# A four-layer attention network on one core: who adds up the causal layer's softmax sums

## The reference

```python
x_ln = _ln(xs, ln1_g, ln1_b)
q = (x_ln @ wq).reshape(b, n, HEADS, DHEAD).transpose(0, 2, 1, 3)
q = q * DHEAD ** (-0.5)
kv = x_ln @ wkv
k, v = (kv[..., :DHEAD], kv[..., DHEAD:])      # one head of keys and values for 8 query heads
sim = jnp.einsum('bhid,bjd->bhij', q, k)
sim = jnp.where(causal, neg, sim)              # causal: key after query
attn = jax.nn.softmax(sim, axis=-1)
out = jnp.einsum('bhij,bjd->bhid', attn, v)
out = out.transpose(0, 2, 1, 3).reshape(b, n, INNER) @ wo
av = _ln(out + xs, ln2_g, ln2_b)
ff = _ln(av, ff_ln1_g, ff_ln1_b) @ ff_w1 + ff_b1
ff = _ln(ff, ff_ln2_g, ff_ln2_b)
ff = jax.nn.gelu(ff, approximate=False) @ ff_w2 + ff_b2
y = ff + av
```

## Time and profile before

| | |
|---|---|
| time, median of 3 runs | 1603.95 us (1603.63 to 1605.78) |
| span of the profiled execution, first to last instruction | 1601.4 us |
| time beside that span | 2.55 us, by the median |
| TensorE busy | 1359.2 us, 85% |
| VectorE busy | 1013.7 us, 63% |
| ScalarE busy | 586.2 us, 37% |
| GpSimd busy | 123.3 us, 8% |
| mean granted TensorE clock | 0.896 of 2.4 GHz |

### The profile page before, as it was taken

One profiled execution on the slowest core, in us unless ns is written; L12 is line 12 of the kernel. 1 busy time (PEld: TensorE's weight loads), 2 busy tenths in 40 slices (PEclk: granted clock), 3 DMA queues, 4 the chain that ended last, 5 costly groups with the idle time before them and its releaser, 6 DMA issues.

```text
span 1601.4 us, 21756 instructions
## 1 busy us (share of the span) xinstructions
PE 1359.2 (85%) x7584; PEld 1024.8 (64%) x7584; DVE 1013.7 (63%) x1837; ACT 586.2 (37%) x797; POOL 123.3 (8%) x314
## 2 busy tenths in 40 slices
PE   4789888859988989876988898896798798889689
PEld 3668654448776865445877776444687687545577
DVE  3656578666565657765646566776565565696655
ACT  3424234524332423533433332353343242245243
POOL 0000011210000002110000000222000000112100
PEclk8799979969978988987998997997898899899799
DMA  4000110000000020000000003000000001200000
GB/s 137 0 27 1 40 41 2 1 1 1 29 1 27 1 67 14 1 1 1 1 29 1 27 0 80 2 1 1 1 0 29 0 1 27 54 1 2 1 1 27
DMA packets 16396, 27.24 MB, mean 17 GB/s; under 512 B 2576, under 2 KB 6800, under 8 KB 16272
## 3 DMA queue, kind: packets, MB, share of 16 engines
q1 hardware_dynamic: 16272, 25.66, 5.8%
HBM read 8.61 MB, written 4.19 MB: 8 GB/s over the span
## 4 chain that ended last, share of the span: by engine, by line
issue 88%; POOL 7%; PE 4%; POOLq 0%; DVE 0%; ACT 0%
PE ring L584 4%; POOL cprobs L555 3%; POOL rstd L539 2%; POOL idle_pool L554 2%; PE ring L654 0%; PE ring L710 0%; POOLq L424 0%; POOLq L538 0%; PE ring L715 0%; ACT h_hi L944 0%; DVE y L1136 0%; POOLq L542 0%; DVE gn_nb L1202 0%; DVE gn_sc L1200 0%; DVE gn_msc L1201 0%
## 5 line engine op out<-in xcount | busy, mean ns | idle before, releaser
L1002 ACT ACTIVATE cprobs<-ring 128x1024 f32<-128x1024 f32 (+1 forms) x192 | 152.1, 812 | 204.8 <-PE ring L830 204.2
L584 PE MATMUL ring<-probsT_hi,vt_hi 128*128 128x512 f32 x384 | 157.3, 410 | 13.6 <-DVE probsT_lo L1086 13.6
L890 ACT ACTIVATE probsT_hi<-ring 128x1024 fp32r<-128x1024 f32 x96 | 98.0, 1026 | 182.1 <-PE ring L654 181.7
L1086 DVE TENSOR_TENSOR probsT_lo<-ring,probsT_hi 128x1024 fp32r<-128x1024 f32 x96 | 116.5, 1221 | 66.2 <-ACT probsT_hi L890 66.2
L806 PE MATMUL ring<-ks,qs 96*128 96x512 f32 (+3 forms) x384 | 144.0, 452 | 14.2 <-DVE part_max L1331 6.1
L584 PE MATMUL ring<-probsT_hi,vt_lo 128*128 128x512 f32 x384 | 153.1, 399 | 0.0
L584 PE MATMUL ring<-probsT_lo,vt_hi 128*128 128x512 f32 x384 | 152.6, 397 | 0.0
L1331 DVE TENSOR_REDUCE part_max<-ring 128x2 f32<-128x1024 f32 (+3 forms) x128 | 127.3, 1017 | 36.1 <-PE ring L810 17.9
L1119 DVE TENSOR_REDUCE neg_max<-ring 128x1 f32<-128x1024 f32 x96 | 116.8, 1221 | 32.7 <-PE ring L584 29.1
L830 PE MATMUL ring<-qs,ks 98*128 98x512 f32 (+3 forms) x384 | 115.0, 394 | 14.7 <-DVE part_max L1331 12.2
L539 POOL TENSOR_TENSOR rstd<-var_eps,half_neg 128x2 f32<-128x2 f32 (+1 forms) x52 | 46.2, 889 | 1026.7 <-DVE var_eps L1197 555.9
(11 more groups left out here) (218 smaller groups left out, 2670.7 us busy)
## 6 DMA issues: line engine op xcount, KB each, us to landing
qs<-q_hi SPq DMA_DIRECT2D x64, 128.0 KB, 2.3
xin<-x_dram SPq DMA_DIRECT2D x4, 1024.0 KB, 4.9
qs<-q_lo SPq DMA_DIRECT2D x32, 128.0 KB, 2.3
out_dram<-y SPq DMA_DIRECT2D x8, 512.0 KB, 3.1
qs<-max_rows SPq DMA_DIRECT2D x64, 4.0 KB
raw_L_wv<-L_wv_dram SPq DMA_DIRECT2D x2, 256.0 KB, 6.1
raw_L_woT<-L_woT_dram SPq DMA_DIRECT2D x2, 256.0 KB, 6.3
raw_L_wqT<-L_wqT_dram SPq DMA_DIRECT2D x2, 256.0 KB, 6.6
```

The costliest lines, as they stand in the source:

```text
L584: ins = mm(out, w, m, start=first and n == 0, stop=last and n == len(every) - 1)
L890: A(dst, flat(name) if src is None else src, ACT.Identity, bias=bias, scale=scale).then_inc(hi_ready, 1)
L1002: A(causal_probs(step, two, n), slot(event_name(e))[:, :, 0:n], ACT.Exp).then_inc(act_read, 1)
L1086: ins = v.tensor_tensor(dst, src, f32(hi), ALU.subtract)
```

## The change

GpSimd adds a block's probability tiles into a new SBUF tile `block_sum` (128 x 4 x 512) as ScalarE delivers them. The products with `ones` leave `values`; a new event `total`, once a block, multiplies `block_sum` with `ones` into bank 1.

- `total(k-1)` stands in the order after the third pair of `exp` of block `k`, directly before the first `values` of block `k`; that of the last block stands after the last `values`. The accumulator's unit is now closed by it, not by the last `values`, so ScalarE's copy and the six `norm` pieces come after it; the `norm` pieces go out two at a time.
- GpSimd takes per `exp` with `jt` of 1 or more: the mask, if on the diagonal, and an add. At `jt` = 1 it adds tiles 0 and 1 (and copies the first columns where tile 1 is narrower); before that it waits until the previous block's `total` has read `block_sum`. Each add waits for the one before it (`block_added`) and for its own mask or exponential.
- ScalarE waits, before it overwrites a `cprobs` buffer, for the add of four steps earlier.
- The scratch for DMA descriptors is set to 1024 bytes, which makes room for `block_sum`.

```diff
@@ causal_schedule
             base += [("exp", k, jt, pair, step) for pair in range(2)]
+            if k and jt == LAG:
+                base.append(("total", k - 1))
             if len(pending) == LAG:
                 base.append(pending.pop(0))
...
             events += [f for at, f in fill[k] if at == i]
-            if divide:
-                events.append(divide.pop(0))
-            if e[0] == "values" and e[1] < k and e[2] == TPH * (blocks[k - 1][1] + 1) - 1:
+            events += divide[:2]
+            divide = divide[2:]
+            if e[0] == "total":
                 divide = norm(k - 1)
...
-    return events + pending + norm(len(blocks) - 1) + [...]
+    return events + pending + [("total", len(blocks) - 1)] + norm(len(blocks) - 1) + [...]
@@ gpsimd
+                        if jt == 0:
+                            continue
+                        total = block_sum[:, 2 * two:2 * two + 2, :]
+                        if jt == 1:
+                            if kk:
+                                wait_filled(pool, b, event_name(("total", kk - 1)))
+                            elif two == 0:
+                                wait_filled(pool, b, event_name(("q2", 1)))
+                        if e in diagonal:
+                            pool.wait_ge(diag_masked, b * DIAG + diag_no[event_name(e)] + 1)
+                        else:
+                            wait_read(pool, b, event_name(e))
+                        new = causal_probs(step, two, n)
+                        if jt == 1:
+                            old = causal_probs(step - 1, two, HALF)
+                            if n < HALF:
+                                pool.tensor_tensor(total[:, :, 0:HALF - n], old[:, :, 0:HALF - n],
+                                                   ones[:, 0:1].unsqueeze(1).broadcast_to([P, 2, HALF - n]), ALU.mult)
+                            pool.tensor_tensor(total[:, :, HALF - n:HALF], old[:, :, HALF - n:HALF], new,
+                                               ALU.add).then_inc(block_added, 1)
+                        else:
+                            pool.wait_ge(block_added, b * ADDS + added[kk, jt - 1, two] + 1)
+                            pool.tensor_tensor(total[:, :, HALF - n:HALF], total[:, :, HALF - n:HALF], new,
+                                               ALU.add).then_inc(block_added, 1)
@@ tensor
+                    if e[0] == "total":
+                        pe.wait_ge(block_added, b * ADDS + added[kk, TPH * (ib + 1) - 1, 1] + 1)
+                        for a in range(4):
+                            last = mm(acc[DH * a:DH * (a + 1), 1, :], ones[:, 0:DH], block_sum[:, a, :],
+                                      start=True, stop=True)
+                        last.then_inc(ring_filled, 1)
...
-                        for bank, w in ((0, v2[:, jt, :]), (1, ones[:, 0:DH])):
-                            for a in range(4):
-                                last = mm(acc[DH * a:DH * (a + 1), bank, HALF - n:HALF], w,
-                                          causal_probs(step, a // 2, n)[:, a % 2, :],
-                                          start=jt == 0, stop=jt == last_jt)
-                        if jt == last_jt:
-                            last.then_inc(ring_filled, 1)
+                        for a in range(4):
+                            mm(acc[DH * a:DH * (a + 1), 0, HALF - n:HALF], v2[:, jt, :],
+                               causal_probs(step, a // 2, n)[:, a % 2, :], start=jt == 0, stop=jt == last_jt)
@@ scalar
+                        if step >= 4:
+                            _, k4, j4, _, _ = step_of[step - 4]
+                            act.wait_ge(block_added, b * ADDS + added[k4, max(j4, 1), two] + 1)
                         A(causal_probs(step, two, n), slot(event_name(e))[:, :, 0:n],
                           ACT.Exp).then_inc(act_read, 1)
-                    elif e[0] == "values" and e[2] == TPH * (blocks[e[1]][1] + 1) - 1:
+                    elif e[0] == "total":
@@ kernel
-    nc = _bacc.Bacc("TRN2", target_bir_lowering=False, num_devices=1)
+    nc = _bacc.Bacc("TRN2", target_bir_lowering=False, num_devices=1, dynamic_dma_scratch_size=1024)
```

More of the change, by code:

```diff
@@ L130, in causal_schedule @@
             events += [f for at, f in fill[k] if at == i]
-            if divide:
-                events.append(divide.pop(0))
-            if e[0] == "values" and e[1] < k and e[2] == TPH * (blocks[k - 1][1] + 1) - 1:
+            events += divide[:2]
+            divide = divide[2:]
+            if e[0] == "total":
                 divide = norm(k - 1)
         assert not divide
-    return events + pending + norm(len(blocks) - 1) + [(e, part) for e in FEED_FORWARD for part in (1, 2)]
+    return events + pending + [("total", len(blocks) - 1)] + norm(len(blocks) - 1) + [(e, part) for e in FEED_FORWARD for part in (1, 2)]
 def evenly(events, places):
@@ L193, in ring_units @@
             for e in causal_schedule():
-                if e[0] == "norm" or len(e) == 2 and e[0] not in FILLS + ("shift",):
+                if e[0] == "norm" or len(e) == 2 and e[0] not in FILLS + ("shift", "total"):
                     continue
@@ L197, in ring_units @@
                     held = True
-                    if e[2] == TPH * (causal_blocks()[e[1]][1] + 1) - 1:
-                        accumulated(event_name(e), "act", (0, 1))
-                        held = e[1] + 1 < len(causal_blocks())
+                elif e[0] == "total":
+                    accumulated(event_name(e), "act", (0, 1))
+                    held = e[1] + 1 < len(causal_blocks())
                 else:
@@ L244, in build @@
     DIAG = len(diagonal)
+    added = {e[1:4]: i for i, e in enumerate(e for e in schedule if e[0] == "exp" and e[2])}
+    ADDS = len(added)
+    step_of = {e[4]: e for e in schedule if e[0] == "exp"}
     last_max = {e[1]: e for e in schedule if e[0] == "max"}
@@ L368, in build @@
         cmax_hi = sb("cmax_hi", [P, 2, TPH, 4], F32R)
+        block_sum = sb("block_sum", [P, 4, HALF])
         idle_act = sb("idle_act", [P, 1])
@@ L403, in build @@
         diag_masked = sem("diag_masked")
+        block_added = sem("block_added")
         dve_step = sem("dve_step")
@@ L788, in causal_layer @@
                 for e in schedule:
-                    if len(e) == 2 and e[0] != "shift":
+                    if len(e) == 2 and e[0] not in ("shift", "total"):
                         stage(b, e)
@@ L795, in causal_layer @@
                     hg, ib = blocks[kk]
-                    if e[0] == "max":
+                    if e[0] == "total":
+                        pe.wait_ge(block_added, b * ADDS + added[kk, TPH * (ib + 1) - 1, 1] + 1)
[3 more added lines that the diff above has]
+                        last.then_inc(ring_filled, 1)
+                    elif e[0] == "max":
                         _, _, ti, _, lo, hi, two = e
@@ L838, in causal_layer @@
                         if jt == 0:
-                            open_unit(b, event_name(e))
+                            open_unit(b, event_name(("total", kk)))
                             if hg == 0:
```

19 lines of the change are left out of this document (12 added, 7 removed).

## The result

The kernel after takes 1756.16 us (median of 4 runs, 1754.0 to 1763.12), the kernel before beside it 1604.87 (4 runs, 1603.63 to 1611.42): a ratio of 1.0962, 95% interval 1.092 to 1.1004, some 151 us slower. The forecast said slower, but 1677.6 with a range from 1588 to 1722. The profiled execution has a span of 1752.9 us at a mean clock of 0.837.

What follows compares the result with a forecast made beforehand. TensorE was taken to bound the end of block 2 and block 3; after the change GpSimd's adds would. 10.3 us plus 8.1 of contention, 18.4 a sample, x 4 = 74 us on 1603.95 gave 1677.6, range 1588 to 1722.

Steps and rivals of the forecast that it cites:

- The add's price: GpSimd adds: 2.1 ns per element plus 0.17 us fixed, so 2.32 us for 1024 elements, 1.78 for 768.
- GpSimd's busy time: Over the profiled execution, a sign of the forecast: from 123 us to some 430.
- `values` waits for masks: GpSimd's masks queue behind its adds and TensorE's values waits for them; TensorE was said to have slack by then.
- contention: Blocks 2 and 3: 30 VectorE instructions beside busy GpSimd, each costing GpSimd 0.27 us, 8.1 us a sample (0 to 13).
- rival B: VectorE waits for whole GpSimd adds of 1.3 to 2.3 us; a sample +23 us, 1696 us; chance 0.17.
- the order at nothing: Norm pieces two at a time were called the same VectorE work, bunched; no cost was charged.
- a small gain in the early blocks: Early gain of 2 us, kept low because values(k,0) newly waits for ScalarE's copy of total(k-1).
- GpSimd is what ends last: Adds of blocks 2 and 3 run from total(1) at 256.4 to total(3) at 324.3, before 314.0: +10.3 us a sample.
- so GpSimd is always fed: ScalarE runs up to four cprobs steps ahead, then waits for block_added, so GpSimd never lacks input.
- rival D: An add is nearly as fast as a one-input pass and hides; 7.5 us a sample gained, 1574 us; chance 0.20.
- Rival A: The forecast itself: GpSimd bounds blocks 2 and 3; own range 1635 to 1725 us; chance 0.47.
- Rival C: TensorE's clock falls because it waits for GpSimd; tg and w2 take some 4 us longer, 1693 us; chance 0.10.

Runs made afterwards that it cites:

- e3: Kernel before, plus multiplications of the adds' sizes on GpSimd at the adds' places, on a tile nobody reads; ratio 1.0803, +128 us.
- e15: e3 with a GpSimd fill, which only writes, in place of each unread multiplication; ratio 1.0397 to the kernel before, +64 us.
- e9: Kernel before with the new order only: no adds, products with ones kept, the last key tile's at the total event; ratio 1.047, +75 us.
- e1: Kernel after with every GpSimd add cut to one column per head, same events and waits; 1651.79 us, ratio 1.032 to the kernel before.
- e4: Kernel after with the products with ones put back in values, their result overwritten by the total; ratio 1.1007 to the kernel before, +161 us.
- e8: Kernel after with two alternating block sums, so adds wait for the total of two blocks earlier; 1752.88 us, ratio 1.093 to the kernel before.
- e12: e1 in the old order: total directly behind the block's last values, division pieces one per event; ratio 1.0101 to the kernel before, +16 us.
- e19: Kernel before with products with ones only for each block's first key tile, 4 sets instead of 24, no adds, old order; ratio 1.0044, +7 us.

## Why the prediction was right or wrong

**Right.** Slower. The add's price, 2.32 us for 1024 elements: 2.33 start to start (267.37 to 269.70), 2.44 by its group; 1.83 for 768 where undisturbed (1.78 said), 1.27 and 0.73 for 512 and 256 (1.25, 0.71). GpSimd's busy time, 406 us for some 430. That `values` waits for masks (7.4 us in the first sample).

**Wrong, the step that failed: contention.** It took from the 0.67 us mask of the earlier trace rows that GpSimd loses 0.27 us a meeting, 8.1 us a sample. GpSimd loses some 2 us a sample (its 1024 element adds take 2.44 on average where 2.38 is undisturbed, one of 768 elements takes 2.62 in place of 1.83, and single masks a little more); VectorE loses the rest of a whole add, an instruction of 0.4 us taking up to 2.5. That was rival B's mechanism, given 0.17, and B too was undersized: it counted six instructions behind `w1`'s root and 4 us of earlier ones, and held against it that "VectorE has 16 us of slack in 272 to 314". The slack didn't help: the divisions stand in VectorE's queue ahead of the maxima and of `w1`'s read, for which TensorE waits at once. e3 puts all of GpSimd's work beside VectorE, with what queues behind it, at 128 us, where the forecast had 32 for contention (8.1 a sample). What comes from GpSimd's reading, the two-input kind above all, is about 64 of these (e3 less e15, whose fills are slightly shorter); the other half falls on copies and scalings, on some 12 us of late roots, and on what was not separated.

The Trainium skill (SBUF — State Buffer, Who interferes with whom) says this nearly as it came: an instruction of VectorE with two SBUF inputs shares a read port with a GpSimd instruction that reads, a copy, cast or scaling in two-port mode contends with any, and the one that comes second is blocked for the other's whole instruction. The traces agree in each point: two-input instructions at 0.42 us beside fills and 0.91 to 1.18 beside multiplications, 2.07 for a scaling beside 2.01 us fills, 1.2 us for the maxima from PSUM and 0.92 for reciprocals in all of them, and on GpSimd's side the 768 element add of 2.62 us, which starts while a VectorE instruction with two inputs runs (338.40 to 339.85).

**Wrong: the order at nothing.** "norm two pieces at a time is the same VectorE work, bunched" is true of the work and false of the time: 33 us in the order alone. The later total and copy, for which the forecast took off no more than a small gain in the early blocks, go with the other 42. Beside the adds the two don't add up: 128 and 75 would be 203, the kernel after has 154. A part of the 49 can be TensorE's relief, which e3 and e9 lack and which gave 24 us between e9 and e1; but with real adds, putting the products back (e4) changed nothing that can be told.

**Wrong: GpSimd is what ends last.** `total(1)` was filled at about 262.5, not 256.4, since TensorE reached it late and at half clock (0.52 between 247 and 263). From there to `total(2)` it took 44.7 us in place of 33.4, and to `total(3)` 43.0 in place of 34.5 (both without contention in the forecast): 6.1 + 11.3 + 8.5 = 25.9 us a sample more than the 324.3, of which 8.1 were given to contention. Block 3's adds did begin when `total(2)` was filled, as said, but the last add of block 2 was done at 303.9 and the total filled only at 307.2, behind TensorE's score products, and with that wait gone (e8) no gain shows. GpSimd idles 4.24, 2.69 and 6.47 us in blocks 2 and 3, always for something that came late through VectorE: "so GpSimd is always fed" was false.

**Wrong: rival D.** A fast add was to give 1574, 7.5 us a sample. e12, with adds of almost no length in the old order, is 16 us slower than before, and e19, with no adds, 7 us: there was nothing to win. That holds for the old order; in the new one fewer products did give something (e1 against e9). "TensorE is the bound (40.07 of 42 us)" was read from busy time; e19 takes seven of block 3's eight sets away and the block isn't shorter. What bounds it there, a chain through VectorE's feed-forward steps or the clock (0.94 between 286 and 314, where it was 1.00), was not tried.

**Rival A's upper end** is also added up wrong: r = 2.6 with the larger fixed part is +23 us a sample without contention, 1697, and +31, 1728, only with the 8.1 us. The measured 1756 lies above both.

**Rival C** isn't supported as the main cause (e4: clock up, time the same), though the clock's share of the loss stays open; a lower clock is what goes with the lost relief in e19.

**Open**: how the overlap of 49 us between order and contention comes about; masks in the kernel after; the clock's share (the mean is 0.837 in the kernel after, 0.896 before); the split of the 42 us into late copy and `values`' wait for it. No version tried is faster than the kernel before by this change.

## What to carry to other kernels

Before work is moved to GpSimd, list every VectorE instruction that will stand beside it and has two SBUF inputs, or is a copy or a scaling on SBUF, and charge each the rest of a whole GpSimd instruction, together with what is queued behind it; an engine's slack in a window doesn't cover a wait ahead of what another engine needs next. To learn what a relief is worth, leave the work out and time that first, in the order in which it will run: here, in the old order, it would have said zero before any add was written. And an order of short instructions between long chains is a cost of its own: two pieces at a time in place of one cost 33 us with the same instructions (beside long adds no such difference showed).

## What the runs showed of the hardware

- With less work TensorE's clock was lower: with 20 of 24 sets of products gone (e19), the granted clock between 248 and 272 us was 0.64 in place of 1.00, 0.79 to 0.82 in the same stretch of the other samples (1.00 before), and over whole executions 0.865 to 0.885 in place of 0.886 to 0.909. Between 212 and 224 us it was higher, 0.91 in place of 0.53.
- A fill on GpSimd, which reads nothing, held up VectorE's scaling of one tensor, 2.07 us each for four in a row where a fill came every 2.01 us, and left two-input products at 0.42 us (e15).
- GpSimd's two-input add of fp32 costs 2.1 ns an element and about 0.2 us, at 256 to 1024 elements a partition (0.73 and 2.33 us). Running back to back it is rarely the one that waits: 29.1 us for twelve of 1024 in the kernel after, 2.44 each where 2.38 is undisturbed; the largest loss seen was 0.8 us, 2.62 for 768 elements.
